# Three tables' rows of group 0 fetched singly by SyncE, and an earlier bridge on TensorE

## The reference

```
e = stack([tbl_f[ids[:, f]] for f in 0..31], axis=1)      # (512, 32, 64)
# CIN, two layers: products of all pairs of rows, per column d, then a weight matrix
z0 = einsum('bhd,bfd->bhfd', e, e)            ; y0 = relu(w0 @ z0 + b0)   # 128 maps
hidden, direct0 = y0[:, :64], y0[:, 64:]
z1 = einsum('bhd,bfd->bhfd', hidden, e)       ; y1 = relu(w1 @ z1 + b1)   # 128 maps
z  = concat([direct0, y1], axis=1).sum(-1)                                # (512, 192)
h  = relu(concat([z, dense_ctx]) @ W_top1 + b_top1)
h  = relu(h @ W_top2 + b_top2)
y  = h @ W_top3
```

## Time and profile before

| | |
|---|---|
| median of three runs | 1070.34 us |
| the profiled execution | 1070.25 us, its span 1068.5 us |
| TensorE busy | 1023.0 us, 96% of the span |
| VectorE busy | 931.2 us, 87% |
| GpSimd busy | 921.0 us, 86% |
| ScalarE busy | 724.6 us, 68% |

### The profile page before, as it was taken

The page is one execution under the profiler, slowest core; times in us unless marked ns, Lnnn a source line. Parts: engine busy times, 40 slices in busy tenths (PEclk is TensorE's granted clock), DMA queues, the critical chain, the costliest instruction groups (busy, mean ns, idle before and its releaser), DMA issues.

```text
span 1068.5 us, 10631 instructions
## 1 busy us (share of the span) xinstructions
PE 1023.0 (96%) x3447; PEld 649.2 (61%) x3447; DVE 931.2 (87%) x610; ACT 724.6 (68%) x794; POOL 921.0 (86%) x300
## 2 busy tenths in 40 slices
PE   2299999999999999999999999999999999999999
PEld 1146556566666666666666666666666666666663
DVE  3079999999998999999999999999989888988881
ACT  5056666677767767776777677677777777777762
POOL 6528777799999999999999999999988988898980
PEclk9999999999999999999999999999999999999999
DMA  6488788778778777887787778777776687677630
GB/s 171 91 208 191 179 196 188 174 189 187 188 179 190 185 176 182 189 194 175 187 191 175 173 189 192 177 191 182 186 167 167 165 190 165 165 170 182 165 73 0
DMA packets 140633, 183.87 MB, mean 172 GB/s; under 512 B 55633, under 2 KB 56273, under 8 KB 140450
## 3 DMA queue, kind: packets, MB, share of 16 engines
q1 hardware_dynamic: 135986, 178.93, 70.7%
q0 software_dynamic: 4096, 4.20, 2.2%
q10 hardware_dynamic: 496, 0.06, 0.0%
HBM read 174.66 MB, written 8.39 MB: 171 GB/s over the span
## 4 chain that ended last, share of the span: by engine, by line
PE 94%; POOL 2%; issue 1%; DVE 1%; ACTq 1%; DMA 1%; ACT 0%; DVEq 0%
PE py L641 43%; PE py L657 16%; PE py L647 16%; PE py L648 16%; POOL emb L341 2%; PE py L662 1%; DVE zf L552 1%; ACTq L449 1%; PE py L676 0%; PE py L713 0%; PE pzS L713 0%; ACTq L221 0%; PE py L683 0%; DMA emb<-in_tbl,idx 0%; DMA idx<-in_ids 0%
## 5 line engine op out<-in xcount | busy, mean ns | idle before, releaser
L351 POOL TENSOR_TENSOR zl<-zf,zh 128x2048 fp32r<-128x2048 f32 x168 | 771.8, 4607 | 87.4 <-ACT zh L413 85.3
L552 DVE TENSOR_TENSOR zf<-xs,hid 128x2048 f32<-128x2048 f32 x256 | 582.9, 2282 | 50.7 <-ACT hid L428 46.8
L641 PE MATMUL py<-zf,wf 128*128 128x512 f32 x1080 | 485.1, 592 | 1.2 <-DVE zf L552 1.2
L413 ACT ACTIVATE zh<-zf 128x2048 fp32r<-128x2048 f32 x185 | 353.5, 1911 | 99.3 <-DVE zf L552 96.0
L641 PEld LDWEIGHTS py<-zf,wf 128*128 128x128 f32 x1080 | 204.3, 189 | 208.5 <-issue 194.7
L647 PE MATMUL py<-zh,wh 128*128 128x512 f32 x740 | 290.0, 392 | 1.3 <-ACT zh L413 1.3
L648 PE MATMUL py<-zh,wl 128*128 128x512 f32 x740 | 289.7, 392 | 0.0
L657 PE MATMUL py<-zl,wh 128*128 128x512 f32 x740 | 228.0, 430 | 0.0
L657 PEld LDWEIGHTS py<-zl,wh 128*128 128x128 f32 x740 | 139.4, 188 | 69.3 <-issue 46.6
L341 POOL DMA_INDIRECT emb<-in_tbl,idx x128 | 149.0, 1164 | 30.3 <-issue 25.5
L647 PEld LDWEIGHTS py<-zh,wh 128*128 128x128 f32 x740 | 139.0, 188 | 34.6 <-ACT zh L413 2.6
(11 more groups left out here) (79 smaller groups left out, 336.1 us busy)
## 6 DMA issues: line engine op xcount, KB each, us to landing
xs<-x_dram SPq DMA_DIRECT2D x512, 256.0 KB, 5.3
xs<-x_dram SPq DMA_DIRECT2D x504, 64.0 KB, 2.1
x_dram<-emb SPq DMA_DIRECT2D x66, 64.0 KB, 5.5
x_dram<-emb SPq DMA_DIRECT2D x22, 96.0 KB, 5.5
emb<-in_tbl,idx POOLq DMA_INDIRECT x128, 4.5
x_dram<-emb SPq DMA_DIRECT2D x4, 384.0 KB
xs<-in_L_rec_w SPq DMA_DIRECT2D x2, 512.0 KB, 4.6
xs<-in_L_rec_w SPq DMA_DIRECT2D x1, 1024.0 KB, 7.5
```

The costliest lines, as they stand in the source:

```text
L351: pool.tensor_tensor(zl[:, q], zf[:, s], zh[:, q].bitcast(F32), ALU.subtract).then_inc(lo["P"], 1)
L413: act.activation(zh[:, q], zf[:, s], ACT.Copy).then_inc(hi, 1)
L552: dve.tensor_tensor(zf[:, slot(u)], left, right, ALU.mult).then_inc(mult, 1)
L641: mm = pe.matmul(y, wf[:, w, h], zf[:, s, h], start=first and h == 0, stop=ends and h == T - 1)
```

## The change

The rows of fields 29 to 31 of block 0 no longer come to `x32` from `emb`. SyncE reads the eight ids of a field into registers, one after the other, and issues for each a DMA of one row of 64 numbers straight from the table (`load_single`). The 24 of them stand in three parts of eight in front of the stores of the first three batches. GpSimd gathers all 32 fields of group 0 as before, since x_dram needs them.

The first group has five batches now: fields 0 to 11, 12 to 19, 20 to 25, 26 to 28 and 29 to 31, and there are five batch semaphores. ScalarE issues eight copies into x32 for each of the first two, then one each for fields 20 to 25, 26 and 27; SyncE issues that of field 28, in front of the store of the fourth batch. TensorE starts its bridging products when the third batch is gathered, and computes five of them in place of two; then it waits for all copies and rows.

```
--- before.py
+++ after.py
@@ -50,11 +50,13 @@
 
 
 
-FIRST_BATCHES = [(0, 0, 12), (0, 12, 12), (0, 24, 5), (0, 29, 3)]
+
+SINGLE = 29
+FIRST_BATCHES = [(0, 0, 12), (0, 12, 8), (0, 20, 6), (0, 26, 3), (0, 29, 3)]
 PER_PERIOD = [[3] * 10 + [2], [2] * 16, [2] * 16]
 LATER_BATCHES = [(c, sum(PER_PERIOD[c - 1][:i]), n) for c in range(1, NC) for i, n in enumerate(PER_PERIOD[c - 1])]
 BATCHES = FIRST_BATCHES + LATER_BATCHES
-BATCH_SEMS = 4
+BATCH_SEMS = 5
 STORES = [sum(min(m, REPEATS) for b, _, m in BATCHES if b == c) for c in range(NC)]
 
 
@@ -197,7 +199,7 @@
         xd_in = [sem("xd_in0"), sem("xd_in1")]
         x0_ready = sem("x0_ready")
         turns_ready, x32_in, x32_last, x_spread = sem("turns_ready"), sem("x32_in"), sem("x32_last"), sem("x_spread")
-        x32_cleared = sem("x32_cleared")
+        x32_cleared, x32_single = sem("x32_cleared"), sem("x32_single")
         x0_first_ready, first_tiles = sem("x0_first_ready"), sem("first_tiles")
         mult, hi, used_whole, used_split = sem("mult"), sem("hi"), sem("used_whole"), sem("used_split")
         lo = dict(V=sem("lo_v"), P=sem("lo_p"))
@@ -246,8 +248,7 @@
                 c, f, m = BATCHES[n]
                 sp.wait_ge(gathered[n % BATCH_SEMS], gathered_count(n))
                 if n == 3:
-                    sp.wait_ge(x32_cleared, 2)
-                    load_x32(sp, 31, x32_last)
+                    load_x32(sp, SINGLE - 1, x32_last)
                 if m < REPEATS:
                     for i in range(m):
                         dst = x_dram[c, f + i:f + i + 1, :]
@@ -298,7 +299,16 @@
                 for j in (0, 2, 1, 3):
                     sp.dma_start(xe[F * j:F * j + F], block_rows(k, j, T)).then_inc(xe_in, 16)
 
+            def load_single(f):
+                for b in range(NS):
+                    row = sp.value_load(idx[b:b + 1, 0, f:f + 1], min_val=0, max_val=tables[f].shape[0] - 1)
+                    sp.dma_start(x32[f:f + 1, D * b:D * b + D], tables[f][bass.ds(row, 1), :]).then_inc(x32_single, 16)
+
+            sp.wait_ge(ids_in, 16)
+            sp.wait_ge(x32_cleared, 2)
             for n in range(len(FIRST_BATCHES)):
+                if SINGLE + n < F:
+                    load_single(SINGLE + n)
                 store_batch(n)
 
             sp.wait_ge(w_turned, 6)
@@ -448,10 +458,10 @@
                 for b in range(NS):
                     act.dma_start(x32[f:f + m, D * b:D * b + D], emb[b:b + 1, 0, f:f + m, :]).then_inc(x32_in, 16)
             act.wait_ge(gathered[2], gathered_count(2))
-            for f in range(24, 29):
+            for f in range(20, 26):
                 load_x32(act, f, x32_in)
             act.wait_ge(gathered[3], gathered_count(3))
-            for f in range(29, 31):
+            for f in range(26, SINGLE - 1):
                 load_x32(act, f, x32_last)
             act.wait_ge(x_spread, 1)
             act.activation(x0_first[:], px0[:], ACT.Copy).then_inc(x0_first_ready, 1)
@@ -676,9 +686,11 @@
                     pe.matmul(bank, wf[:, 0, i % T], wf[:, 1].rearrange("p t n -> p (t n)"), start=True, stop=True)
 
             pe.wait_ge(turns_ready, 1 + T + 2)
-            pe.wait_ge(x32_in, 16 * (2 * NS + 5))
-            warm_up(2, py1[:, 0])
-            pe.wait_ge(x32_last, 16 * 3)
+            pe.wait_ge(gathered[2], gathered_count(2))
+            warm_up(5, py1[:, 0])
+            pe.wait_ge(x32_in, 16 * (2 * NS + 6))
+            pe.wait_ge(x32_last, 16 * (SINGLE - 26))
+            pe.wait_ge(x32_single, 16 * NS * (F - SINGLE))
             for n, y in enumerate([px0[:]] + xd_first + [xt_first]):
                 pe.matmul(y, spreads[:, n], x32[:], start=True, stop=True).then_inc(x_spread, 1)
             main(("P", 0))
```

## The result

The changed kernel takes 1100.87 us (median of five, 1099.97 to 1102.67), the kernel before 1070.34 (median of five): the ratio is 1.0284 [1.027, 1.0299]. The forecast, 1068.9 in a range from 1067 to 1080, was wrong by 32 us.

A forecast was written before the change was run, and what follows sets the result against it. TensorE was taken as the bound, so only an earlier start of its unbroken work counts: 1.85 us gained less 0.5 for idle time, rows free, gain 1.4, 1070.34 - 1.4 = 1068.9 us; range 1067 to 1080.

The forecast's parts named there:

- 24 rows one by one: SyncE's queue before the first stores: 24 single-row fetches at 1.13 us each, cost 0, hidden beside the gathers.
- r: SyncE's time per single row: forecast 1.13 us, from issue 0.63, hand-overs 0.15, register instructions 0.09, load 0.26.
- SyncE's gaps: SyncE's free time from 12.96 us and between its batch stores (7.8, 9.9, 7.5 us), claimed to take the row work.
- upper bound: Highest price of one SyncE row: 3.4 us, summed as 0.79 + 0.15 + 0.78 + 1.65.
- rival 1: SyncE becomes the bound, last store and loads late: 1078 us; chance beyond 0.3% slower 0.36.
- Break-even: SyncE's row price of 1.25 us, up to which the extra eats only the 0.83 us and the copy's slack.
- the forecast's own rate: Beyond 1.25 us a SyncE row, each further tenth costs 24 x 0.1 = 2.4 us of total time.
- the px copy waits longer than 0.68 us: Sign in ScalarE's queue: its first px copy, at about 58 us, waits for a DMA longer than the earlier 0.68 us.
- SyncE's moved copy: SyncE's 0.79 us x32 copy goes before batch 3's store, moving the last store and later loads 0.83 us earlier.
- What that is worth: Start of TensorE's unbroken work: 1.85 us earlier (bounds 0 and 1.85), VectorE's products following the first A product.
- rival 3: Nothing of the lead is passed on: loads land as late, clock falls, 0.15 us slower, 1070.5 us; chance 0.12.
- TensorE's idle time: Before the first A product: 5.0 us idle, perhaps slow passes behind, 0 to 1.2 us lost, 0.5 taken.

The follow-up runs named there:

- e1_hold: Changed kernel, but GpSimd begins its gathers only when the first eight single rows have landed: 1111.6 us.
- e7_plain: Changed kernel, but plain transfers of rows 0 to 127 of each table replace group 0's gathers by id: 1074.85 us.
- e4_bridge: Changed kernel without single rows (five batches and five bridging products stay; fields 29 to 31 copied as before): 1070.31 us, ratio 0.9993 to the kernel before.
- e8_spaced: Changed kernel with a waited-for fill of 1024 columns after each gather of group 0, so gathers stand 2.19 us apart: 1097.47 us.
- e5_sync: Changed kernel, but only table 31's eight rows are fetched singly by SyncE, fields 29 and 30 by copies: 1082.81 us, ratio 1.0113.
- e6_act: Changed kernel, but only table 31's eight rows fetched singly, by ScalarE ahead of its x32 copies instead of SyncE: 1093.68 us, ratio 1.0219.
- e12_tiny: Kernel before, without single rows, plus 48 one-column fills on VectorE beside the gathers: 1071.45 us.
- e13_both: Changed kernel with its 24 single rows by SyncE, plus 48 one-column fills on VectorE: 1100.34 us.
- e2_static: Changed kernel, but the 24 rows are plain transfers from fixed addresses, no register loaded: 1072.02 us, ratio 1.0021.
- e3_loads: Changed kernel with ids loaded and checked, but the transfers use fixed addresses: 1093.32 us.

## Why the prediction was wrong

1. **The step that failed is "24 rows one by one".** It summed r = 1.13 us and set it against SyncE's gaps "covered by the gathers". The gathers were no cover; they were the cause. Beside them the first eight rows cost 36.5 us instead of 9.0 (e1_hold), 27.5 more, and that is most of the 30.88 by which the loads came late. The upper bound, 3.4 us a row, did not hold either (4.7 from the first load at 13.4 to 50.8), since it priced the instructions each by itself and no effect of a neighbour. The outcome is rival 1's, the last store and the loads late, but its price, 1078 us, was 23 short for the same reason.
2. **Even undisturbed, r was too small, and that alone would have cost the gain.** Measured 1.25: the load 0.49 instead of 0.26, the rest 0.76 instead of 0.87 (the trace has six instructions for a row, where the list under the change shows five: a second step of the address). Break-even was put at 1.25. What I left out is the first rows behind each store: their loads take up to 1.1 us in the changed kernel. With them, e7_plain's 24 rows cost 1.38 each (14.0 to 49.6 less two pairs of stores of 1.25). By the forecast's own rate that is 24 x 0.13 = 3.1 us, and 1.0 for the start at 14.0 instead of 12.96: 4.1; it was 4.7 us slower. The Trainium skill's price ("DMA: Bandwidth & Descriptors", "Latency and other measured facts": a floor of about 600 ns) lies above the 0.49 us of these runs and its other price ("Runtime: NRT & Kernel Launch", "Instruction fetch mechanics": about 200 ns) below; for the load itself the larger was the nearer one.
3. **Right:** bridging from 38.29 (38.05 forecast), ScalarE's copies done by 44.1 (43.4), the last chain runs over the loads, the px copy waits longer than 0.68 us (1.75), the steady part keeps its length. The lead of 1.83 us in e4_bridge against 1.85 is right in the number only: it came by another way than over SyncE's moved copy.
4. **"What that is worth" was still too much:** VectorE's products did not go on following the first A product. In e4_bridge the next block's load landed no earlier, VectorE came to a stop, and nothing is gained (-1.8 to +0.2 us). That is near rival 3, whose 1070.5 fits, partly by luck: a load landed no earlier, though a block later than it had it. "TensorE's idle time" was misplaced: 1.24 us before the first A product instead of 5.0, with quick passes behind; idle time with slow passes behind it stood before the spreading products. That the moved copy alone is worth its 0.83 us, no run shows.

What stays open is why the instructions are held up. Shown: it needs back-to-back gathers by id (e1_hold, e8_spaced; e7_plain for the 6 us in which its transfers lie beside the rows), touches SyncE, ScalarE and VectorE (e5_sync, e6_act, e12_tiny), each for itself (e13_both), grows with the number of instructions (e2_static, e3_loads), begins only after some have passed, and ends some 5 us after the last gather where they stand 1.25 us apart. A held-up instruction shows 0.70 us at its start, at its end, or at both. Start and end are what a trace records, and every execution timed here was recorded, so it can't be excluded that the recording is what is held up. The Trainium skill ("NOTIFIC — the notification-queue block", "7.1 Overflow: three behaviours, one of which stalls the engine") describes counted stalls in which the path for such records throttles an engine. No run here shows that count, and none is without a recording.

## What to carry to other kernels

Price an instruction that you put beside another engine's dense stream by a row from that same stretch, and where the stretch has none, treat "free, since the engine is idle" as the assumption that decides. Place many small instructions where the stream is not (e1_hold's first eight rows), and count them: one transfer of eight rows costs one instruction, eight rows by id cost 48. And before an earlier start is worth anything, look whether the transfers behind it start earlier too.

## What the runs showed of the hardware

- Beside GpSimd's gathers 1.25 us apart, instructions of 0.02 to 0.5 us on SyncE, ScalarE and VectorE took one or two steps of 0.70 us; with gathers 2.19 us apart, none of SyncE's rows was held up; plain transfers about 0.5 us apart held up none of them either.
- A load of an id from SBUF into a register: 0.49 us; behind SyncE's stores up to 1.1 us.
- A whole row by id (six instructions): 1.25 us, of which the transfer's issue is 0.27.
